# Attention scores formed transposed in float32: block maxima through DRAM, partial denominators on GpSimd

## What is computed

```
a = layer_norm(ctx) * gamma + beta            # 32 x 375 x 512
Q, K, V = x @ Wq.T, a @ Wk.T, a @ Wv.T        # split into 16 heads of 32
scores = Q K^T * 32**-0.5                     # per head 112 x 375, masked where mask is False
attn = softmax(scores)                        # over the 375 context rows
out = x + tanh(gate) * ((attn V) @ Wo.T)
```

## Time and profile before

| | us |
|---|---|
| median of 3 runs | 1139.86 (1137.56 to 1142.44) |
| span of the profiled execution, first to last instruction | 1134.9 |
| its own time beside the span | not listed apart; the median of the runs stands 5.0 above the span |
| PE busy | 1100.3 (97%) |
| DVE busy | 861.4 (76%) |
| ACT busy | 679.0 (60%) |
| POOL busy | 565.0 (50%) |
| granted PE clock, mean over the span | 0.987 |

### The profile page before, as it was taken

The page is one execution under the profiler, slowest core; times in us unless marked ns, Lnnn a source line. Parts: engine busy times, 40 slices in busy tenths (PEclk is TensorE's granted clock), DMA queues, the critical chain, the costliest instruction groups (busy, mean ns, idle before and its releaser), DMA issues.

```text
span 1134.9 us, 28841 instructions
## 1 busy us (share of the span) xinstructions
PE 1100.3 (97%) x9614; PEld 921.6 (81%) x9614; DVE 861.4 (76%) x2438; ACT 679.0 (60%) x1811; POOL 565.0 (50%) x745
## 2 busy tenths in 40 slices
PE   9799899999999999999999999999999999999997
PEld 8798788878888888888888888888888887888885
DVE  4643888887877788888787788888787778887764
ACT  2414565656666666666666666666666666666653
POOL 1344746555555566655455566655554566655100
PEclk9899899999999999999999999999999999999997
DMA  9453223222333233323333333323333333331000
GB/s 270 168 152 70 69 73 72 55 76 74 83 85 85 72 85 73 66 64 75 77 85 85 80 77 77 70 56 75 77 85 85 82 75 76 67 67 45 10 17 17
DMA packets 53010, 89.55 MB, mean 79 GB/s; under 512 B 15184, under 2 KB 35664, under 8 KB 52976
## 3 DMA queue, kind: packets, MB, share of 16 engines
q1 hardware_dynamic: 52400, 88.19, 31.8%
q10 hardware_dynamic: 576, 0.92, 0.3%
HBM read 81.66 MB, written 7.44 MB: 79 GB/s over the span
## 4 chain that ended last, share of the span: by engine, by line
PE 72%; DVE 16%; DMA 5%; issue 4%; POOL 1%; ACT 1%; SPq 1%; DVEq 0%; POOLq 0%
PE bank L690 43%; PE bank L747 14%; PE bank L847 6%; DVE shared_f L668 6%; PE bank L770 6%; DVE stats L574 4%; DVE shared_f L649 3%; PE bank L712 2%; DMA qT<-in_wkT 2%; DMA row_stats<-row_stat 1%; DMA rows<-in_ctx 1%; DVE mv L577 1%; POOL cn L404 1%; ACT shared_f L513 1%; DMA stat_bc<-row_stats 0%
## 5 line engine op out<-in xcount | busy, mean ns | idle before, releaser
L404 POOL TENSOR_TENSOR cn<-cn,stat_bc 128x375 f32<-128x375 f32 x256 | 258.8, 1043 | 387.4 <-DMA stat_bc<-row_stats 371.1
L513 ACT ACTIVATE shared_f<-shared_f,ntop 112x375 f32<-112x375 f32 x512 | 306.3, 601 | 14.3 <-DVE ntop L649 14.1
L690 PE MATMUL bank<-shared_r,w_k 128*128 128x376 f32 x1536 | 295.9, 342 | 0.0
L690 PE MATMUL bank<-w_v,shared_r 128*125 128x512 f32 x1152 | 291.7, 402 | 0.1
L649 DVE CUSTOM_DVE_ANT_0 shared_f<-bank,mask_b 112x375 f32<-112x375 f32 x512 | 258.6, 543 | 32.1 <-PE bank L770 30.8
L690 PEld LDWEIGHTS bank<-shared_r,w_k 128*128 128x128 f32 x1536 | 260.4, 190 | 0.3
L747 PEld LDWEIGHTS bank<-ident,shared_f 112*125 112x125 f32 x1536 | 199.1, 190 | 67.9 <-issue 27.9
L690 PEld LDWEIGHTS bank<-w_v,shared_r 128*125 128x125 f32 x1152 | 206.7, 186 | 46.1 <-issue 0.5
L668 DVE TENSOR_SCALAR shared_f<-shared_f,rden 112x375 f32<-112x375 f32 x512 | 240.3, 531 | 4.5
L747 PE MATMUL bank<-ident,shared_f 112*125 112x112 f32 x1536 | 222.1, 281 | 20.2 <-DVE shared_f L668 19.6
L536 ACT ACTIVATE shared_f<-bank 125x448 f32<-125x448 f32 x256 | 139.0, 543 | 166.8 <-PE bank L747 166.8
(11 more groups left out here) (49 smaller groups left out, 816.4 us busy)
## 6 DMA issues: line engine op xcount, KB each, us to landing
rows<-in_ctx SPq DMA_DIRECT2D x32, 750.0 KB
cn<-in_ctxT SPq DMA_DIRECT2D x32, 750.0 KB, 12.2
stat_bc<-row_stats SPq DMA_DIRECT2D x32, 375.0 KB, 4.4
xy<-in_x SPq DMA_DIRECT2D x32, 224.0 KB, 2.5
out<-xy SPq DMA_DIRECT2D x32, 224.0 KB, 2.3
shared_f<-in_xT SPq DMA_DIRECT2D x7, 896.0 KB, 8.9
mask_u<-in_mask SPq DMA_DIRECT2D x32, 41.0 KB, 3.1
qT<-in_wqT SPq DMA_DIRECT2D x4, 256.0 KB, 5.5
```

The source lines that it names most:

```text
L404: last = pool.tensor_tensor(chunk, chunk, stat_bc[:, w, :], op)
L513: last = act.activation(prob[0:T, r % 2, h, :], prob[0:T, r % 2, h, :], ACT.Exp, bias=ntop[0:T, r % 2, h:h + 1], scale=-1.0, accum_out=den ...
L690: last = pe.matmul(dst, l, m, start=(start and k == 0), stop=(stop and k == len(pairs) - 1))
```

## The change

Scores are formed with the context rows on the partitions: for each third of 125 context rows and each head, a float32 matmul with K as the stationary operand (32 rows, 125 columns) and Q as the moving one (112 columns). K and Q are not split any more (one ACT copy for K, one POOL copy for Q). The weights come out in the form that the weighted sum reads, so the transposes and their copies go. The maximum over the context rows is now a maximum over partitions. It is formed in steps: ACT copies the scores out with the mask as a bias (three copies of 125 x 448 into `prob`, rows 125 to 127 preset very low); DVE reduces each block of 32 partitions with a transposing reduction (three, 128 x 448); SP stores the 128 x 42 maxima to DRAM and loads them back so that every block of 32 partitions sees all 12 candidates (`x4`, 128 x 168); DVE reduces these to 128 x 14, spreads them with a block transpose to 128 x 448 and subtracts them from the three thirds; ACT takes the exponentials in place. There is no sum along the row any more: POOL adds the three thirds (two additions of 125 x 448 in each slot), and PE sums over partitions with four matmuls against ones. The division moves behind the weighted sum, once a batch on DVE (`normalise`). The layer norm on POOL is spread over three slots, the statistics on DVE over two.

An item (four heads of a batch) is now spread over more slots: scores in slot n on PE; copy, block maxima and round trip in slot n+1; final maximum, subtraction, exponential and weighted sum in slot n+2; addition of the thirds and denominators in slot n+3.

```diff
 @block.sync
+            def exchange_maxima(i, r):
+                sync.wait_ge(quad_max, i * LOOP + r)
+                sync.dma_start(row_max.rearrange("t (q k) -> q t k", q=HC), rmax[:, :]) \
+                    .then_inc(max_stored, 16)
+                wait_apart(sync, max_stored, i * (16 * LOOP) + r * 16)
+                sync.dma_start(x4[:, :], bass.AP(
+                    tensor=row_max.tensor, offset=0,
+                    ap=[[0, HC], [HC * ST * BLK, 32], [1, HC * ST * BLK]])).then_inc(ld_max, 16)
             def slot(i, r):
                 c, u = divmod(r, KT)
+                if live(i, LOOP, r - 1, SLOTS):
+                    exchange_maxima(i, r)
+                if u == 0:   store_stats(i, c + 3) ; load_x(i, c - 1)
+                if u == 2:   load_stats(i, c + 3) ; load_ctx(i, c + 3)
+                if u == 3:   load_rows(i, c + 5) ; out[c - 2] <- xy
...
 @block.gpsimd
+            def sum_chunks(i, r):
+                q = (r - 3) % NB
+                wait_apart(pool, exp_done, i * (LOOP * ST) + (r - 2) * ST)
+                if behind(i, LOOP, r - 3):
+                    wait_apart(pool, pv_mm, i * LOOP + (r - 2))
+                pool.tensor_tensor(psum[0:SP_, :], prob[0:SP_, q, 0, :], prob[0:SP_, q, 1, :],
+                                   ALU.add).then_inc(sum_step, 1)
+                wait_apart(pool, sum_step, i * LOOP + (r - 2))
+                pool.tensor_tensor(psum[0:SP_, :], psum[0:SP_, :], prob[0:SP_, q, 2, :],
+                                   ALU.add).then_inc(sum_done, 1)
+            # slot: [u == 3: copy_q, copy_bias]; sum_chunks; u == 0: center; u == 1: divide;
+            #       u == 2: affine; u == 3: row_statistics
...
 @block.scalar
+            # slot: scores_out(r - 1) (3 copies); weighted_out(r - 3) (1 copy); u == 0: oT high;
+            #       K copy (r + 1); 3 exponentials (r - 2); context_hi; V copy
...
 @block.vector
+            def row_maximum(i, r):
+                dve.wait_ge(ld_max, i * (16 * LOOP) + (r - 1) * 16)
+                dve.tensor_reduce(top[:, :], x4[:, :].rearrange("p (a k) -> p k a", k=BLK),
+                                  AX.X, ALU.max).then_inc(top_done, 1)
+                dve.wait_ge(top_done, i * LOOP + (r - 1))
+                dve.transpose(spread.rearrange("p (k a) -> p k a", a=32),
+                              top[:, :].unsqueeze(2).to_broadcast([128, BLK, 32])) \
+                    .then_inc(spread_done, 1)
+            def quadrant_maxima(i, r):
+                for j in range(ST):
+                    dve.wait_ge(s_out, i * (LOOP * ST) + ((r - 1) * ST + j + 1))
+                    last = dve.tensor_reduce(
+                        rmax[:, BLK * j:BLK * j + BLK],
+                        prob[:, (r - 1) % NB, j, :].rearrange("p (k a) -> p k a", a=32),
+                        AX.X, ALU.max, apply_transpose=True)
+                last.then_inc(quad_max, 1)
+            def subtract_maximum(i, r):
+                dve.wait_ge(spread_done, i * LOOP + (r - 1))
+                for j in range(ST):
+                    dve.tensor_tensor(prob[0:SP_, (r - 2) % NB, j, :], prob[0:SP_, (r - 2) % NB, j, :],
+                                      spread[0:SP_, :], ALU.subtract).then_inc(sub_done, 1)
             def slot(i, r):
+                    row_maximum(i, r)
+                    quadrant_maxima(i, r)
+                    subtract_maximum(i, r)
+                # u == 3: normalise (5 instructions); u == 0: oT low; u == 1: bn_rows;
+                # u == 2: bn_rows, bn_join; context_lo; u == 1: result
...
 @block.tensor
+            def scores(i, r):
+                for j in range(ST):
+                    for h in range(HC):
+                        part = slice(HD * h, HD * h + HD)
+                        last = pe.matmul(bank[h][0:SP_, T * j:T * j + T],
+                                         kT[part, r % 2, SP_ * j:SP_ * j + SP_],
+                                         qs[part, c % 2, u, :], start=True, stop=True)
+            def weighted_sum(i, r):
...
+                    for h in range(HC):
+                        last = pe.matmul(bank[PB][HD * h:HD * h + HD, T:2 * T], ones[0:SP_, :],
+                                         psum[0:SP_, T * h:T * h + T], start=True, stop=True)
+            # slot: project_k(r + 1); project_v or, for u == 1, output; scores(r);
+            #       weighted_sum of item r - 2 with the denominators of item r - 3
-            transpose_probs, group_2 (PE), transposed (ACT), transposed_1 (DVE), split_q,
-            convert_mask (POOL), the low parts of K and Q, the special order at the end
```

More of the change, by code:

```diff
@@ L42 @@
 LOOP = 2 * KT
+HT = HC * T
+BLK = HT // 32
+NB = 4
 SCALE = float(HD) ** -0.5
 EPS = 1e-5
-HIGHEST = 3.4e38
+LOWEST = -3e38
 WARM_UP = 7
@@ L209, in slots @@
         def slots(engine, slot, first=-1, last=SLOTS // LOOP + 1):
-            for i in range(first, 1):
+            for i in range(first, 2):
                 for r in range(LOOP):
                     slot(i, r)
-            with engine.Fori(1, SLOTS // LOOP - 2) as i:
+            with engine.Fori(2, SLOTS // LOOP - 3) as i:
                 for r in range(LOOP):
                     slot(i, r)
-            for i in range(SLOTS // LOOP - 2, last):
+            for i in range(SLOTS // LOOP - 3, last):
                 for r in range(LOOP):
@@ L340, in _ @@
+                if u == 3:
+                    if live(i, 2, c + 5, B) and behind(i, 2, c + 2):
+                        load_rows(i, c + 5)
+                    if live(i, 2, c - 2, B):
+                        wait_apart(sync, y_done, i * 2 + (c - 1))
+                        sync.dma_start(out[i * 2 + (c - 2), :, :], xy[0:T, c % 2, :]) \
+                            .then_inc(stored[c % 2], 16)
             slots(sync, slot)
@@ L396, in row_statistics, with center @@
                 pool.sem_inc(row_stat_done, 1)
-            def normalise(i, c):
+            def center(i, c):
                 wait_apart(pool, ld_stat, i * 32 + (c + 1) * 16)
                 wait_apart(pool, ld_ctx[c % 2], (i + c // 2 + 1) * 16)
[L401 to L410, removed]
@@ L412, in slot @@
-            def slot(i, r):
[L413 to L419, removed]
-                if live(i, 2, c + 1, B):
-                    split_q(i, c + 1)
-                    convert_mask(i, c + 1)
-                if live(i, 2, c + 3, B) and (not isinstance(i, int) or 2 * i + c >= 0):
-                    row_statistics(i, c + 3)
+                for k in range(KT):
+                    last = pool.tensor_tensor(cn[:, c % 2, k, :], cn[:, c % 2, k, :],
+                                              stat_bc[:, 0, :], ALU.add)
@@ L435, in _ @@
                     .then_inc(pad_done, 1)
-            pool.wait_ge(q_out, KT)
+            pool.wait_ge(pad_done, 2)
+            for q in range(NB):
+                if q == NB - 1:
+                    pool.wait_ge(mask_mm, 1)
+                pool.memset(prob[96:128, q, :, :], LOWEST).then_inc(low_done, 1)
+            pool.wait_ge(low_done, NB)
+            pool.wait_ge(q_out, GROUPS * KT)
             slots(pool, slot)
@@ L539, in _ @@
+                if j is not None and live(i, 2, vc, B):
+                    act.wait_ge(v_mm, i * (2 * ST) + (vc * ST + j + 1))
+                    act.activation(v_sb[0:SP_, vc % 2, j, :], bank[VO[r % 2]][0:SP_, :], ACT.Copy) \
+                        .then_inc(v_done, 1)
             slots(act, slot)
@@ L578, in statistics @@
                 last.then_inc(stats_done, 1)
+            def statistics(i, c):
+                bn_rows(i, c, range(ST))
+                bn_join(i, c)
             def weight_lo(n, raw, dst):
@@ new lines, in weighted_sum, with transpose_mask, slot @@
+                last.then_inc(pv_mm, 1)
+            def transpose_mask():
+                pe.wait_ge(mask_f_done, 1)
+                pe.wait_ge(q_out, GROUPS * KT)
+                for j in range(ST):
+                    last = pe.transpose(bank[PB][0:SP_, B * j:B * j + B],
+                                        mask_f[0:B, SP_ * j:SP_ * j + SP_], ident[0:B, 0:B])
+                last.then_inc(mask_mm, 1)
+            def slot(i, r):
+                if live(i, LOOP, r + 1, SLOTS):
+                    project_k(i, r)
+                vc, j = v_item(r)
+                if j is not None and live(i, 2, vc, B):
+                    project_v(i, r, vc, j)
+                if r % KT == 1 and live(i, 2, r // KT - 2, B):
+                    output(i, r)
+                if is_slot(i, r, -1):
+                    transpose_mask()
+                if live(i, LOOP, r, SLOTS):
+                    scores(i, r)
+                if live(i, LOOP, r - 2, SLOTS + 1):
+                    if is_slot(i, r, 2):
+                        pe.wait_ge(mask_out, 1)
+                    weighted_sum(i, r)
```

596 lines of the change are left out of this document (312 added, 284 removed).

## The result

| | before | after |
|---|---|---|
| median, us | 1138.99 (1137.56 to 1142.44, 4 runs) | 1267.99 (1264.35 to 1271.20, 4 runs) |
| ratio, 95% interval | 1 | 1.112 [1.109, 1.116] |
| profiled span, us | 1134.9 | 1262.4 |
| PE, DVE, ACT, POOL busy, us | 1100, 861, 679, 565 | 1075, 933, 646, 772 |
| granted PE clock | 0.987 | 0.933 |

The account below looks back on a forecast made before the run. The exchange of maxima was taken to bound the changed kernel: 28 batches at 4.1 us more (115), the last four 10, the ends 8, together 133 on 1134.9, plus 5 from span to median: 1273 us; range 1100 to 1400.

Parts of the forecast that it names:

- the ring: Each slot holds one maxima round trip plus DVE's part ahead of it, not overlapped: 8.2 us a quiet slot; chance 0.55.
- rival 4: POOL binds, its additions slowed by a quarter beside DVE: 9.0 us a slot, about 1300 us; chance 0.08.
- DVE ahead of the store, 2.7: DVE's small reduction, completion wait, spreading transpose and three block reductions before the maxima are stored: 2.7 us a slot.
- Round trip 5.5: Block maxima from DVE through SP's store and load back to DVE's start: 5.5 us, bounds about 4.5 and 7.5.
- Behind `rows` 2.6 us more: Once a batch the next store of maxima waits in SP's queue behind `rows` and `out`: 2.6 us more.
- A batch 35.9: Four slots of 8.2 us plus 3.1 for other transfers in the queue: 35.9 us against 31.8 before.
- DVE busy 6.2 a slot, hidden: DVE's work in a slot, its share of once-a-batch steps included: 6.2 us, less than the 6.4 before.
- PE 6.9 a slot, 80% of the span: PE without transposes, with float32 scores and denominators: busy 6.9 us a slot, about 80% of the span.
- rival 5: PE loses its clock through waiting and needs about 11 us a slot: near 1530 us; chance 0.05.
- POOL 6.9: POOL's additions, layer norm, statistics, copies and waits: 27.7 us a batch, 6.9 a slot, as much as PE.
- The ends, 8 us: Extra time outside the batches: 3 us in the prologue and 5 us after the last scores (about 25 against 20).
- the estimate from the Trainium skill: Exchange transfers on 4 engines: the load of `x4` some 0.8 us more a slot, time near 1370; not in the sum.

Follow-up runs that it names:

- e1: Changed kernel with the maxima exchanged once, for the first item only, and stale maxima subtracted after that: 1096.8 us, ratio 0.963.
- e2: Changed kernel with SP storing the block maxima twice, each time waiting for the landing, before loading them: 1545.4 us, ratio 1.355.
- e4: Changed kernel with DVE forming an item's block maxima before the previous item's final maximum, with two buffers for loaded maxima: 1151.1 us, ratio 1.009.
- e6: Changed kernel with the thirds summed on PE (12 matmuls instead of 4) and POOL's two additions removed: 1273.1 us, ratio 1.118.
- e5: Changed kernel with the load of `rows` issued as two loads, of 112 and 13 partitions, on SP: 1215.1 us, ratio 1.066.
- e7: Changed kernel with block maxima formed before the previous item's final maximum and the thirds summed on PE: 1136.1 us, ratio 0.999.
- e3: Changed kernel with the loads of `rows` issued by ACT at the end of its slot 3 instead of by SP: 1357.1 us, ratio 1.189.
- e10: Kernel before the change, with the load of `rows` in two parts of 112 and 13 partitions: 1113.5 us, ratio 0.978.

## Why the prediction was right

The mechanism was the one forecast, near its forecast price. Three runs show that the ring sets the slot: without the exchange the loss is gone (e1), one more store in the ring is paid in full (e2), and opening the ring gives 117 us back (e4). POOL's additions, rival 4, are ruled out by e6. Its steps:

- *DVE ahead of the store, 2.7*: 2.73. The sum held although its parts did not: the reduction of 168 took 0.45 (0.33 forecast), the step from it to the spreading transpose 0.03 (0.17 forecast), and the three block reductions 1.58 from start to start (1.62 forecast). A transposing reduction ran at the pitch of a copy, in the middle of the bounds of half and twice.
- *Round trip 5.5*: 5.3 in the quiet slot (2.24 and 3.02). From the last block reduction's end to the store's issue it is 0.03 (0.2 forecast). This term and the 0.2 from landing to DVE's start came from no row; when the load lands no trace shows, so the second stays unmeasured inside the 3.02. The slot is 8.0 where 8.2 was forecast. (The upper bound of 10.5 for the slot was too low by its own terms: 7.5 and, with reductions at twice the pitch, 4.2 make 11.7.)
- *Behind `rows` 2.6 us more*: 2.4 in the slot shown (1.9 on the store, 0.5 on the load). Over 25 batches the store behind `rows` took 4.1 on the average. The row it was argued from, the 6.9 us of `row_stats`, shows less than was read from it: `cn`, another 750 KB, was issued between `rows` and that store (at 604.25), and both were ahead of it. e5 and e7 show the wait behind `rows` itself. e5 gave 1.2 a batch back of the 2.4; where the other half went is open.
- *A batch 35.9*: 35.7, from slots of 10.4, 8.0, 8.6 and 8.8. Over the whole run the small reduction starts 127 intervals apart from 125.1 to 1242.7, 8.80 each; 8.98 was forecast for batches with transfers.
- *DVE busy 6.2 a slot, hidden*: mis-sized. It is 28.7/4 = 7.2. `context_lo` took 0.92 on the average where it had taken 0.55, the subtractions 0.71, `normalise`'s multiplication 1.52, all two-operand instructions in SBUF that ran beside POOL. In one slot of four (34 of 128; after `normalise`, and POOL adding and normalising) DVE came late by itself and the load had landed. This did not show in the time, since that slot was 8.8 instead of 8.2 while the quiet ones were a little shorter. I had weighed the contention as a slowing of POOL; it was DVE that slowed, while POOL's additions kept their 1.2.
- *PE 6.9 a slot, 80% of the span*: 7.6 (30.45/4) and 85%. K 2.2, V 2.9 and scores 0.85, from start to start of the next, hold at the full clock. The weighted sum does not: its three parts are released by three exponentials one after another, and it takes 1.3 (606.38 to 607.67) where 0.71 was forecast. The denominators take 0.31 (0.24 forecast). And the clock fell for parts of a batch (0.94 over 200 us), which rival 5 had held possible. None of this showed in the time, since PE has slack in the ring.
- *POOL 6.9*: 24.05/4 = 6.0; the additions cost 1.2 each as forecast, the layer norm and the statistics less.
- *The ends, 8 us*: from the last scores (1225.2) to the end it is 37 us, against about 20 of before; 25 was forecast. Each step waits for the one before it, and PE is slower (4.85 us for the output product, 2.95 in mid-span; the granted clock from 1250 to 1260 us is 0.66), and the slot structure adds `normalise` behind one more round trip. This made up for the somewhat shorter slots.

The ends were 12 us longer than forecast and the 127 intervals 16 us shorter (1118 against 1133). So that the forecast came within 6 us of the result is in part luck: two errors of opposite sign, each larger than what was left. By the estimate from the Trainium skill ("DMA: Bandwidth & Descriptors", "Why a DMA increments its semaphore by 16 and not by 1"), `x4` was to take 0.8 us more than by my rows, and the kernel about 1370 us. The quiet load took 0.1 more (3.02 to DVE's start; I had 2.9), so that estimate was too high. Its rule on the number of engines was what the experiments needed: 112 and 13 partitions instead of 125 made `rows` short (e5).

## What to carry to other kernels

The same round trip cost 171 us where the step that starts the next one stood behind the wait for the last, and some 54 us where it did not (e4 against e1). Before judging busy shares, go once around each ring: from a wait, through what is queued behind it, back to the same wait. Here putting the producing step ahead of the waiting one was worth 117 us with the same work on the engines and one more small buffer. And a small transfer that is waited for should be judged with the large ones ahead of it in its queue: `rows` with its 125 partitions in one load was an expensive shape here, for the store behind it and in the prologue.

## What the runs showed of the hardware

- A small store with nothing ahead takes 2.2 us from its issue to the issue of a transfer that waited for it; the load of 84 KB behind it 3.0 until DVE starts. Behind `rows`, at different distances, the same store takes 4.1 or 6.7.
- A large load on ACT's queue, issued 0.2 us ahead of a small one on SP's, slowed the small one from 3.0 us to 9.0 (e3).
- `rows`, 750 KB on 125 partitions, moves at a DMA share of 0.29 and keeps the queue for 9 us; as 112 and 13 partitions the share is 0.93 and the queue is free after 5 us (changed kernel, e5).
- A two-operand DVE instruction on 125 x 448 in SBUF takes 0.6 us alone; three of them took 1.65, and 3.2 to 3.8 when POOL worked beside them all the time (e1, e7). The transposing reduction kept its 0.6 beside POOL (602.81 in the changed kernel).
- Splitting one load by partitions, 112 and 13, gave a kernel that is bound by PE 25 us, 10 of them in the prologue (e10).
